# Routed attention and expert kernel: weight scaling and row turning moved between slots, expert steps written out with transposing loads

## The chip, the cores and the metric

The kernel runs on one core of one Trainium2 chip. The metric is the time of one execution on the device, in microseconds (us), less is better.

## What is computed

```python
h = tok(x)                 # 32 batches of 125 tokens x 192; the 88 with the best score are kept
h = h + attn(layernorm(h)) # 12 heads of 16, values rounded to whole steps, integer softmax
h = h + ffn(layernorm(h))

def ffn(x):                # 16 experts, each 192 -> 2 x 192 -> 192, 4 of them for each of 2816 tokens
    t = rmsnorm(x) * scale
    vals, idx = top_k(t @ gate_w.T + gate_b, 4)
    full_w = scatter(softmax(vals) / 4, idx)
    h = swiglu(einsum('th,ehf->tef', t, w1) + b1)
    y = einsum('tei,eih->teh', h, w2) + b2
    return x + einsum('teh,te->th', y, full_w) * 4
```

## The kernel before, in words

All is written out by hand: each engine has one list of instructions and semaphores, and each executes its own list in order. There are three stages.

**Start.** x is loaded, scored and the kept tokens are gathered (to about 95 us).

**Attention slots.** The tokens are NT = 24 tiles of 128 rows, three tiles to a quad of four batches (NQ = 8). `tile_slots` calls `slot(st, ...)` for st = 0 to 29 on every engine. A slot takes one tile's scores through the integer softmax: VectorE makes S_w (L1227), ScalarE S_g (L827), VectorE S_rho and S_pow (L1264, L1267), ScalarE a Square (L851), VectorE S_e and its sum (L1302, L1306), ScalarE Ln and Exp (L876, L881), VectorE S_ratio, S_rb and S_p (L1244 to L1253, in the next slot), TensorE transposes of S_p (L1593, L1598), ScalarE copies to pTs (L858, L861), TensorE pO (L1631), ScalarE o8 (L837), POOL a cast to oq (L651), TensorE the projection (L1618), VectorE the residual (L1277). Other work is laid into the slots by i = st % 3:
- q, k and v of the next quad. `project_qk` (L1486) fills bank pX, `quant_qk` (L771) on ScalarE empties it, and POOL casts it (L610). Six of these (qk 0 to 5) lie at i = 0 and 1, the v parts at i = 2.
- Expert weights in pairs: SP loads a pair into stage0 or stage1 (L442), `scale_pair` on ScalarE scales them (L720 to L726, at i = 1), `high_bias` and `high_w1` (L733 to L744) make the float16 high parts, POOL the low parts (`low_pair`, L537, at i = 0).
- Routing of a finished quad: `norm_rows` (L1128), `high_rows` (L784), low halves on POOL (L313, L314), then at st = 7 + 3q (i = 1) `turn_rows` (L1530) transposes the rows into pX in two parts, which VectorE copies (`evac_rT`, L1142); `last_rows` (L791) on ScalarE; the gate's product `gate_rows` (L1545) and `top_experts` (L1151 to L1163); and at i = 2 the ranks (L1555) and `find_slots`. POOL sends the rows to their places in `region` in HBM (L622), 12 DMAs to a quad.

All who use bank pX take it in the order of `fill_order`: each filler waits until the one before was emptied (`xr_drained`). How many sends POOL makes in a slot is given by `room`:

```python
room = 5 if st == NT else len(queue) if st > NT else (1, 6, 5)[st % 3]
```

**Expert stage.** `region` holds the rows by expert in blocks of STEP = 256. NS = 59 steps each take one block: SP loads it (`load_step`, L477 to L481, four buffers xb), TensorE transposes it into tp_ps (L1690), ScalarE copies that to xTb and its tail to tEb (L929, L930), TensorE makes the hidden layer, three windows of five products (L1681), ScalarE applies the gate function (L920, L923), VectorE clamps the other half (L1379, L1382) and multiplies (L1410), ScalarE and VectorE split the result into high and low parts (L914, L915, L1389, L1390), TensorE makes ten products (L1705), ScalarE copies them out (L908), POOL sends the result rows with two indirect DMAs (L686) to `expert_rows`. VectorE works out their addresses from 16 words behind each row (L1398, L1414). `step_slots` writes the first 16 steps and the last ones out and runs the 40 between as a loop of UNROLL = 8; TensorE reads the experts' numbers at the start of every eight (`load_experts`).

At the end the result rows are loaded again and summed on VectorE (L1428).

## Time and profile before

| | |
|---|---|
| runs | 790.51 us median of 3 (790.07 to 792.04) |
| profiled execution | 788.26 us, its span 786.5 us |
| busy, share of the span | PE 52%, PE weight loads 36%, DVE 79%, ACT 70%, POOL 56% |
| attention slots | about 98 to 499 us |
| sends of rows, tables | to 540 us |
| expert stage | 545 to 745 us |
| result rows summed | 751 to 783 us |

PE is TensorE's matmul, PEld its weight load, DVE is VectorE, ACT ScalarE, POOL GpSimd, SP SyncE; SPq is SP's DMA queue. A row of a timeline gives the start, the duration and the instruction (line, output <- inputs, shape), and in brackets how long the engine stood idle before it and for whom. "arena" is one large buffer in which many tiles lie.

### The profile page before, as it was taken

How to read it: one execution, taken by the hardware profiler on the slowest of the kernel's cores; microseconds unless marked ns; L12 is line 12 of the kernel's file. 1: busy time of each engine (PE TensorE's matmuls, PEld its weight loads, DVE VectorE, ACT ScalarE, POOL GpSimd, SP SyncE). 2: the span in 40 equal slices, each digit the busy share in tenths (PEclk: the TensorE clock that was granted, in tenths of full speed). 3: DMA queues.
4: the chain of work that ended last, by engine and by line, in shares of the span. 5: the costliest groups of instructions: out<-in, count | busy, mean ns of one | idle time of the engine just before them, and what ended most of it. 6: DMA issues, size and time to landing. Idle time of an engine off the chain costs nothing. (4 is left out here: it accounts for less than half of the span.)

```text
span 786.5 us, 16017 instructions
## 1 busy us (share of the span) xinstructions
PE 408.7 (52%) x4141; PEld 279.9 (36%) x4142; DVE 624.7 (79%) x1844; ACT 546.8 (70%) x914; POOL 437.5 (56%) x542
## 2 busy tenths in 40 slices
PE   0377545553434444544534332322999999999400
PEld 0123213232222232322312222211777777878300
DVE  3686478989599598796995988775998888888378
ACT  0235289998878788778788876426998899889300
POOL 9543263735417558378287386774366566666600
PEclk9999655555555555555555555555999999999655
DMA  8479999688201102002000001123344443333095
GB/s 185 52 166 321 319 318 296 200 264 258 60 1 39 58 24 72 25 24 85 11 24 30 29 5 49 64 79 90 94 126 122 118 121 111 108 114 98 3 380 209
DMA packets 102400, 93.47 MB, mean 119 GB/s; under 512 B 14822, under 2 KB 96493, under 8 KB 102338
## 3 DMA queue, kind: packets, MB, share of 16 engines
q1 hardware_dynamic: 88938, 72.87, 33.5%
q0 software_dynamic: 10272, 17.70, 6.5%
q10 hardware_dynamic: 3128, 2.16, 0.9%
q8 instruction: 28, 0.46, 0.2%
q14 instruction: 34, 0.28, 0.1%
...
## 5 line engine op out<-in xcount | busy, mean ns | idle before, releaser
L686 POOL DMA_INDIRECT expert_rows<-stage,dest x118 | 116.3, 985 | 85.8 <-DVE dest L1414 64.8
L622 POOL DMA_INDIRECT region<-rows,slots x60 | 65.4, 1090 | 17.8 <-issue 14.0
L1486 PE MATMUL pX<-arena,WA 128*128 128x384 f16 x86 | 35.3, 514 | 66.2 <-ACT arena L771 63.5
L537 POOL TENSOR_TENSOR w1s<-stage,w1s 128x384 f16<-128x384 f32 (+8 forms) x72 | 56.4, 784 | 9.6 <-ACT w1s L744 4.6
L1593 PE MATMUL pP<-idb,S_p 128*88 128x128 bf16 x192 | 25.8, 315 | 65.5 <-DVE S_p L1253 65.5
L1705 PE MATMUL pX<-w2s,stage 128*128 x472 | 56.8, 251 | 4.3 <-ACT stage L908 2.6
L651 POOL CAST oq<-o 128x384 bf16<-128x384 int8 x24 | 19.3, 804 | 68.7 <-ACT o L837 68.5
L1593 PEld LDWEIGHTS pP<-idb,S_p 128*88 128x88 bf16 x192 | 21.9, 191 | 70.8 <-DVE S_p L1253 68.8
L610 POOL CAST arena<-arena 128x384 bf16<-128x384 int8 x42 | 25.5, 614 | 38.1 <-ACT arena L771 37.8
L914 ACT ACTIVATE stage<-arena 128x512 f16<-128x512 f32 x59 | 37.2, 630 | 13.4 <-DVE arena L1410 12.2
L827 ACT ACTIVATE S_g<-S_w,kf 128x1056 int16<-128x1056 uint16 x24 | 30.3, 1264 | 21.6 <-DVE S_w L1227 21.6
L1410 DVE SCALAR_TENSOR_TENSOR arena<-arena 128x256 f32<-128x256 f32 x118 | 44.2, 416 | 0.0
L622 POOL DMA_INDIRECT region<-arena,slots x36 | 37.9, 1052 | 10.6 <-issue 8.7
L1705 PEld LDWEIGHTS pX<-w2s,stage 128*128 128x128 f16 x472 | 39.3, 98 | 10.6 <-issue 8.2
L1379 DVE TENSOR_SCALAR arena<-pP 64x256 f32<-64x256 f32 x59 | 25.1, 426 | 20.9 <-PE pP L1681 19.4
L1690 PE MATMUL pO<-idh,arena 128*128 128x128 f16 x354 | 30.0, 222 | 20.8 <-DMA arena<-region 19.4
L537 POOL TENSOR_TENSOR w2s<-stage,w2s 128x384 f16<-128x384 f32 (+2 forms) x24 | 37.9, 1579 | 1.9
L1302 DVE SCALAR_TENSOR_TENSOR S_e<-S_sq,kf,S_pow 128x1056 f32<-128x1056 f32 x24 | 33.7, 1405 | 5.3 <-ACT S_sq L851 5.3
L1264 DVE SCALAR_TENSOR_TENSOR S_rho<-S_g,kf,S_w 128x1056 int16<-128x1056 int16 x24 | 36.8, 1533 | 0.0
L1142 DVE COPY early<-pX 128x768 f16<-128x768 f16 (+1 forms) x16 | 7.3, 457 | 37.0 <-PE pX L1530 37.0
L1244 DVE TENSOR_TENSOR S_ratio<-S_sq,esum 128x1056 uint16<-128x1056 f32 x24 | 33.0, 1375 | 3.9 <-ACT S_sq L881 3.9
L1508 PE MATMUL pS<-arena 32*96 32x88 bf16 (+1 forms) x576 | 32.5, 274 | 4.4 <-ACT S_u L777 2.7
...
## 6 DMA issues: line engine op xcount, KB each, us to landing
...
expert_rows<-stage,dest POOLq DMA_INDIRECT x118
```

The source lines that it names most:

```text
L537: pool.tensor_tensor(ws[rows, min(kind + 1, 3), two, to:to + width], st[rows, :, at:at + width], ws[rows, kind, two, to:to + width], ALU.s ...
L622: pool.indirect_dma_start(region_rows, bass.IndirectOffsetOnAxis(ap=slots[q % 3][:, i, m:m + 1], axis=0), rows[q % 3][:, i, :].bitcast(I16 ...
L686: pool.indirect_dma_start(y_dram, bass.IndirectOffsetOnAxis(ap=dest[(st - 7) % 8][:, j:j + 1], axis=0), ysb[b][:, j, :], None, bounds_chec ...
L914: act.activation(av[b][:, 0:3:2, :], act_f[b], ACT.Copy).then_inc(s["hi_ready"], 1)
L1244: dve.tensor_tensor(S_ratio[:, :, :], S_sq[:, :, :], esum1[:, :].unsqueeze(2).broadcast_to([128, H, KEEP]), ALU.mult).then_inc(s["ratio_re ...
L1264: dve.scalar_tensor_tensor(S_rho[:, :, :], S_g[:, :, :], k(K_X), S_w[:, :, :], ALU.mult, ALU.subtract).then_inc(s["rho_ready"], 1)
L1302: dve.scalar_tensor_tensor(S_e[:, :, :], S_sq[:, :, :], k(K_KK), S_pow[:, :, :].bitcast(BF16), ALU.add, ALU.mult).then_inc(s["e_ready"], 1)
L1410: dve.scalar_tensor_tensor(act_f[f][part, m, :], gsig[r][part, m, :], G7, lin[r][part, m, :], ALU.min, ALU.mult).then_inc(s["a_ready"], 1)
L1486: ins = pe.matmul(bank[:, 0:384], W[:, 128 * c:128 * c + 128], xT[:, kind, :], start=kind == 0, stop=kind == 2)
L1508: ins = pe.matmul(pS[rows, j, KEEP * c:KEEP * c + KEEP], qT[r][blk, c, at:at + m], kT[r][blk, c, MAIN * b:MAIN * b + KEEP], start=True, st ...
L1593: ins = pe.transpose(pP[0:KEEP, 0, 128 * h:128 * h + 128], S_p[:, h, :].bitcast(BF16), idb[:, :])
L1705: ins = pe.matmul(y_ps[:, j, :], lhs, w2s[:, kind, bass.ds(k_, 1), :].rearrange("p o f -> p (o f)"), start=n == 0, stop=n == 4)
```

## The change

In the attention: `scale_pair` is split into `scale_bias`, now at i = 0, and `scale_w1`, now at i = 2; qk 3 is emptied right behind qk 2; the routed rows take bank pX before qk 4 and the gate before qk 5; VectorE's bn_stats stands between its two copies of the turned rows; POOL sends 1, 4 and 7 rows instead of 1, 6 and 5. In the expert stage: the loop is gone, all steps are written out, and the experts' numbers are read into eight registers once; the tile is loaded by a transposing DMA straight into xTb, which has eight buffers (four in the tiles of the softmax, four in the arena), and the 16 words behind each row by a second DMA, two rows to a partition; TensorE's transposes, their bank and ScalarE's large copy are gone, the tail is copied from xTb; VectorE's two clamps become one operation, and so do its two products; the two small sums with an accumulator become one operation, and a reduce takes the place of the cast. Since a partition now has two neighbouring rows' addresses, the high and low parts are written with even rows first.

```diff
-xb = [carve([2, ROW], I16, 2) for _ in range(4)]
+meta = [carve([2, 16], I16, 2) for _ in range(UNROLL)]
+xTa = [carve([3 * STEP], I16, 2) for _ in range(4)]
...
-xTb = [buf[:, :, :].rearrange("p a b -> p (a b)").bitcast(F16)[:, 0:3 * STEP].rearrange("p (k n) -> p k n", k=3)
-       for buf in (S_g, S_rho, S_pow, S_ratio)]
+xTb = [buf[:, :, :].rearrange("p a b -> p (a b)").bitcast(I16)[:, 0:3 * STEP].rearrange("p (k n) -> p k n", k=3)
+       for buf in (S_g, S_rho, S_pow, S_ratio)] + [buf.rearrange("p (k n) -> p k n", k=3) for buf in xTa]
...
-tp_ps = pO[:, 0:3 * STEP // 2].bitcast(F16).rearrange("p (k n) -> p k n", k=3)
...
         order += [(st, "qk", 2), (st, "qk", 3)] if i == 1 else []
-    if nxt:
-        order += [(st, "x", 2)] if i == 0 else [(st, "qk", 4)] if i == 1 else [(st, "v", 1)]
+    if nxt and i != 1:
+        order += [(st, "x", 2)] if i == 0 else [(st, "v", 1)]
     if quad_at(st, RANK) is not None:
...
         order += [("rows", quad_at(st, TURN), m) for m in range(2)]
+    if nxt and i == 1:
+        order += [(st, "qk", 4)]
+    if quad_at(st, GATE) is not None:
+        order += [("gate", quad_at(st, GATE))]
     if nxt and i < 2:
         order += [(st, "qk", 5 * i)]
-    if quad_at(st, GATE) is not None:
-        order += [("gate", quad_at(st, GATE))]
 return {name: 11 + n for n, name in enumerate(order)}
...
-room = 5 if st == NT else len(queue) if st > NT else (1, 6, 5)[st % 3]
+room = 5 if st == NT else len(queue) if st > NT else (1, 4, 7)[st % 3]
...
 COLUMNS = ((0, FF, 0), (FF + CA, 2 * FF, FF), (FF, FF + CA, 2 * CA))
-def step_slots(eng, begin, slot):
-    last = NS // UNROLL
-    for st in range(2 * UNROLL):
-        if st % UNROLL == 0:
-            begin(st // UNROLL)
+def step_slots(eng, slot):
+    for st in range(NS + 7):
         slot(st, st, st // UNROLL)
-    with eng.Fori(2, last) as it:
-        begin(it)
-        for u in range(UNROLL):
-            slot(2 * UNROLL + u, it * UNROLL + u, it)
-    for st in range(UNROLL * last, NS + 7):
-        if st % UNROLL == 0:
-            begin(st // UNROLL)
-        slot(st, st, st // UNROLL)
 ROUTE_CONSTS = 38
+def by_half(full):
+    return full.rearrange("p k (n j) -> p k j n", j=2)
 def active(st, lag):
...
 def load_step(st, p, it):
-    b = st % 4
+    b = st % UNROLL
     if st >= NS:
         return
-    k = sp.value_load(tabi[0:1, 1, bass.ds(p + 8, 1)], min_val=0, max_val=NBLK)
-    if st >= 4:
-        sp.wait_ge(s["tp_filled"], p - 3)
-        sp.wait_ge(s["dest_ready"], p - 3)
-    sp.dma_start(xb[b], region[bass.ds(k, 1)].rearrange("o (j p) c -> p (o j) c", p=128)).then_inc(step_loaded[b], 16)
+    _, (k,) = nc.values_load_multi_w_load_instructions(
+        tabi[0:1, 1, st + 8:st + 9], [mybir.EngineType.SP], min_val=0, max_val=NBLK,
...
+    if st >= UNROLL:
+        sp.wait_ge(s["hl_ready"], p - (UNROLL - 1))
+        sp.wait_ge(s["te_copied"], p - (UNROLL - 1))
+        sp.wait_ge(s["dest_ready"], p - (UNROLL - 1))
+    sp.dma_start(xTb[b], region[bass.ds(k, 1), :, 0:2 * C].rearrange("o n c -> (o n) c"),
+                 transpose=True).then_inc(step_loaded[b], 16)
+    sp.dma_start(meta[b], region[bass.ds(k, 1), :, 2 * C:ROW].rearrange("o (p j) c -> p (o j) c", j=2),
+                 allow_slow_non_contiguous=True).then_inc(meta_loaded[b], 16)
 for b in range(4):
...
+def scale_w1(r):
+    st = stage_in[r]
...
         quant_qk(q + 1, 2, fill(st, "qk", 2))
-    if i == 1 and st <= 19:
-        scale_pair(q * 80 + 80 * (3 - (st // 3 + 1) % 2), (st // 3 + 1) % 2)
+    if nxt and i == 1:
+        quant_qk(q + 1, 3, fill(st, "qk", 3))
     if i == 2 and st <= 20:
+        scale_w1((st // 3 + 1) % 2)
         high_bias(q + 1, q * 2 + 2, (st // 3 + 1) % 2)
...
         high_w1(q * 2, st // 3 % 2)
+    if i == 0 and st <= 18:
+        scale_bias(q * 80 + 80 * (3 - (st // 3 + 1) % 2), (st // 3 + 1) % 2)
     if st < NT:
...
         act.activation(S_sq[:, :, :], S_rho[:, :, :], ACT.Square, bias=k(K_NB2)).then_inc(s["sq_ready"], 1)
-    if nxt and i == 1:
-        quant_qk(q + 1, 3, fill(st, "qk", 3))
     if 1 <= st <= NT:
...
                        ACT.Copy).then_inc(s["pTs_ready"], 1)
-    if nxt and i == 1:
-        quant_qk(q + 1, 4, fill(st, "qk", 4))
     if i == 2 and st // 3 + 2 < NQ:
...
         last_rows(quad_at(st, TURN))
+    if nxt and i == 1:
+        quant_qk(q + 1, 4, fill(st, "qk", 4))
     if quad_at(st, COEFFS) is not None:
...
     if active(st, 3):
-        act.wait_ge(s["a_ready"], p * 2 - 4)
+        act.wait_ge(s["a_ready"], p - 2)
         if st >= 7:
             act.wait_ge(s["mm2_done"], p - 6)
-        act.activation(av[b][:, 0:3:2, :], act_f[b], ACT.Copy).then_inc(s["hi_ready"], 1)
-        act.activation(avE[b][0:CB, :], act_f[b][0:CB, 1, :], ACT.Copy).then_inc(s["ave_ready"], 1)
+        act.activation(av[b][:, 0:3:2, :].rearrange("p k (j n) -> p k j n", j=2), by_half(act_f[b]),
+                       ACT.Copy).then_inc(s["hi_ready"], 1)
+        act.activation(avE[b][0:CB, :].rearrange("p (j n) -> p j n", j=2), by_half(act_f[b])[64:128, 1],
+                       ACT.Copy).then_inc(s["ave_ready"], 1)
     if active(st, 2):
-        act.wait_ge(s["h_ready"], p * 3 - 5)
+        act.wait_ge(s["h_ready"], p * 2 - 3)
         if st >= 4:
         act.activation(gsig[r][:, 0, :], hidG[r], ACT.Gelu_apprx_sigmoid,
                        scale=1.0 / (XS * WS)).then_inc(s["gs_ready"], 1)
-        act.activation(gsig[r][0:CB, 1, :], hidC[r][0:CB, :], ACT.Gelu_apprx_sigmoid,
+        act.wait_ge(s["h_ready"], p * 2 - 2)
+        act.activation(gsig[r][64:128, 1, :], hidC[r][0:CB, :], ACT.Gelu_apprx_sigmoid,
                        scale=1.0 / (XS * WS)).then_inc(s["gs_ready"], 1)
     if active(st, 0):
-        act.wait_ge(s["tp_filled"], p + 1)
+        act.wait_ge(step_loaded[u], it * 16 + 16)
         if st >= 4:
-        act.activation(xTb[st % 4], tp_ps, ACT.Copy).then_inc(s["tp_drained"], 1)
-        act.activation(tEb[st % 4][0:CB, :], tp_ps[0:CB, 2, :], ACT.Copy).then_inc(s["te_copied"], 1)
+            act.wait_ge(s["hl_ready"], p - 3)
+        act.activation(tEb[st % 4][0:CB, :], xTb[u][0:CB, 1, :].bitcast(F16), ACT.Copy).then_inc(s["te_copied"], 1)
 for q in range(NQ):
...
         norm_x(q + 2)
-    if quad_at(st, TURN) is not None:
-        evac_rT(quad_at(st, TURN), 1)
     if 3 <= st < NT + 3:
...
         dve.bn_stats(stb[:, m, :], xsel[:, m, :]).then_inc(s["stats2"], 1)
+    if quad_at(st, TURN) is not None:
+        evac_rT(quad_at(st, TURN), 1)
     if quad_at(st, COEFFS) is not None:
...
 def expert_values(st, p, it):
...
-        dve.wait_ge(s["h_ready"], p * 3 - 4)
+        dve.wait_ge(s["hl_ready"], p - 1)
+        dve.wait_ge(s["gs_ready"], p * 2 - 2)
...
-            dve.wait_ge(s["a_ready"], p * 2 - 6)
-        dve.tensor_scalar(lin[r][0:CB, 1, :], hidC[r][64:128, :], -6.0 * XS * WS, 8.0 * XS * WS, ALU.max,
-                          ALU.min).then_inc(s["l_done"], 1)
-        dve.wait_ge(s["h_ready"], p * 3 - 3)
-        dve.tensor_scalar(lin[r][:, 0, :], hidL[r], -6.0 * XS * WS, 8.0 * XS * WS, ALU.max,
+            dve.wait_ge(s["a_ready"], p - 3)
+        dve.tensor_scalar(lin[r], hidLC[r], -6.0 * XS * WS, 8.0 * XS * WS, ALU.max,
...
-        dve.tensor_tensor(av[g][:, 1, :], act_f[g][:, 0, :], av[g][:, 0, :], ALU.subtract).then_inc(s["lo_ready"], 1)
-        dve.tensor_tensor(av[g][64:128, 2, :], act_f[g][0:CB, 1, :], av[g][0:CB, 2, :],
+        parts, halves = av[g].rearrange("p k (j n) -> p k j n", j=2), by_half(act_f[g])
+        dve.tensor_tensor(parts[:, 1], halves[:, 0], parts[:, 0], ALU.subtract).then_inc(s["lo_ready"], 1)
+        dve.tensor_tensor(parts[0:CB, 2], halves[64:128, 1], parts[64:128, 2],
...
-        dve.wait_ge(step_loaded[b], it * 32 + 16 * ((u - 1) // 4) + 16)
+        dve.wait_ge(meta_loaded[m], it * 16 + 16 * ((u - 1) // UNROLL) + 16)
...
-        for j in range(2):
-            ins = dve.scalar_tensor_tensor(rkj[o][:, j, :], meta[:, j, 0:TOPK], own[:, bass.ds(p - 1, 1), j],
-                                           meta[:, j, TOPK:2 * TOPK], ALU.is_gt, ALU.add,
-                                           accum_out=rk[o][:, j:j + 1])
-        ins.then_inc(s["rk_done"], 1)
+        dve.scalar_tensor_tensor(rkj[o][:, :, 0:TOPK], tags[:, :, 0:TOPK], own[:, st - 1:st],
+                                 tags[:, :, TOPK:2 * TOPK], ALU.is_gt, ALU.add).then_inc(s["rk_done"], 1)
...
-        for m, part in enumerate((slice(0, 128), slice(0, CB))):
-            dve.wait_ge(s["gs_ready"], p * 2 + (m - 3))
-            dve.wait_ge(s["l_done"], p * 2 - 2)
-            dve.scalar_tensor_tensor(act_f[f][part, m, :], gsig[r][part, m, :], G7, lin[r][part, m, :], ALU.min,
-                                     ALU.mult).then_inc(s["a_ready"], 1)
+        dve.wait_ge(s["l_done"], p - 1)
+        dve.scalar_tensor_tensor(act_f[f], gsig[r], G7, lin[r], ALU.min, ALU.mult).then_inc(s["a_ready"], 1)
...
-        dve.tensor_copy(dest[(st - 1) % 8][:, :], rk[o][:, :]).then_inc(s["dest_ready"], 1)
...
+        with nc.allow_low_precision(reason="sums of whole numbers below two to the power of 24"):
+            dve.tensor_reduce(dest[(st - 1) % 8][:, :], rkj[o][:, :, :], AX, ALU.add).then_inc(s["dest_ready"], 1)
...
-    if nxt and i == 1:
-        project_qk(q + 1, 4, fill(st, "qk", 4))
...
+    if nxt and i == 1:
+        project_qk(q + 1, 4, fill(st, "qk", 4))
...
+    if quad_at(st, GATE) is not None:
+        gate_rows(quad_at(st, GATE))
...
-    if quad_at(st, GATE) is not None:
-        gate_rows(quad_at(st, GATE))
...
-        pe.wait_ge(s["tp_drained"], p - 1)
+        b = (st - 2) % UNROLL
+        pe.wait_ge(step_loaded[b], it * 16 + 16 * ((u - 2) // UNROLL) + 16)
...
-            for n, (kind, rhs) in enumerate(((0, x3[:, 0, :]), (0, x3[:, 1, :]), (1, x3[:, 0, :]),
-                                             (2, x3[:, 2, :]), (3, tail[:, :]))):
+            for n, (kind, rhs) in enumerate(((0, x3[:, 0, :]), (0, x3[:, 2, :]), (1, x3[:, 0, :]),
+                                             (2, x3[:, 1, :]), (3, tail[:, :]))):
...
-            ins.then_inc(s["h_ready"], 1)
-    if active(st, 0):
-        pe.wait_ge(step_loaded[b], it * 32 + 16 * (u // 4) + 16)
-        if st >= 1:
-            pe.wait_ge(s["te_copied"], p)
-        for j in range(2):
-            for kind, lo in enumerate((0, 2 * CA, CA)):
-                ins = pe.transpose(tp_ps[:, kind, 128 * j:128 * j + 128], xb[b][:, j, lo:lo + 128].bitcast(F16), idh[:, :])
-        ins.then_inc(s["tp_filled"], 1)
+            ins.then_inc(s["hl_ready" if dst is hidL[r] else "h_ready"], 1)
```

What moves, first on ScalarE in a slot with i = 1 (slot 10): behind o8 come before

```order
L837 ACTIVATE o8<-pO,kf 128x384
L771 ACTIVATE arena<-pX,qkB,qkA 128x384
L720 ACTIVATE stage1<-stage1 64x2x192
L721 ACTIVATE stage1<-stage1 64x2x192
L722 ACTIVATE stage1<-stage1,one_ws 64x2x192
L724 ACTIVATE stage1<-stage1 128x2x384
L726 ACTIVATE stage1<-stage1,fs 128x2x384 x2
L851 ACTIVATE S_sq<-S_rho,kf 128x1056
L771 ACTIVATE arena<-pX,qkB,qkA 128x384
L858 ACTIVATE pTs<-pP 88x1024
L861 ACTIVATE pTs<-pP 88x512
L771 ACTIVATE arena<-pX,qkB,qkA 128x384
```

and of the change

```order
L847 ACTIVATE o8<-pO,kf 128x384
L781 ACTIVATE arena<-pX,qkB,qkA 128x384 x2
L864 ACTIVATE S_sq<-S_rho,kf 128x1056
L869 ACTIVATE pTs<-pP 88x1024
L872 ACTIVATE pTs<-pP 88x512
L801 ACTIVATE tEr<-early 64x384
L781 ACTIVATE arena<-pX,qkB,qkA 128x384
L887 ACT_TABLE_LOAD
```

The arena rows from pX are qk 2, 3 and 4: the six scalings are gone from between the first two, and qk 4 now comes behind the copy to tEr.

On TensorE in the same slot (qk 3, S_p, qk 4, rows, projection) before

```order
L1486 MATMUL pX<-arena,WD 128x384
L1593 MATMUL pP<-idb,S_p 88x128 x8
L1598 MATMUL pP<-idb,S_p 88x128 x4
L1486 MATMUL pX<-arena,WA 128x384 x2
L1486 MATMUL pX<-arena,WD 128x384
L1530 MATMUL pX<-idh,rows0 128x128 x9
L1618 MATMUL pP<-WpT,oq 128x192 x3
```

and of the change

```order
L1492 MATMUL pX<-arena,WD 128x384
L1599 MATMUL pP<-idb,S_p 88x128 x8
L1604 MATMUL pP<-idb,S_p 88x128 x4
L1536 MATMUL pX<-idh,rows0 128x128 x9
L1492 MATMUL pX<-arena,WA 128x384 x2
L1492 MATMUL pX<-arena,WD 128x384
L1624 MATMUL pP<-WpT,oq 128x192 x3
```

The transposes of the routed rows (rows0) have moved ahead of qk 4.

## Rows read from the trace of the kernel before

**Rows 1.** Busy time by stretches: stretch, busy time of each engine (xinstructions), PEclk, DMA share, GB/s.
```profile
600.00:650.00 50.00, 46.99 (x484) 38.57 (x484) 42.42 (x173) 44.37 (x109) 30.25 (x32) 1.00 0.41 118
```

**Rows 2.** Chain of waits of the expert stage, shares by line.
```profile
by line: PE pS L1681 30.4%; PE pX L1705 20.6%; PE pP L1681 14.0%; PE pO L1690 8.1%; issue 6.3%; DVE xsel L1428 3.9%; DMA w1s<-expert_rows 2.0%; DVE arena L1410 1.2%; ACT avE L915 1.1%; DMA arena<-region 1.1%; DMA region<-rows,slots 1.1%; AC
```

**Rows 3.** Timeline of ScalarE, slots 10 to 12: start us, us, instruction [idle before].
```profile
251.14 1.27 ACT L827 ACTIVATE S_g<-S_w,kf 128x1056 int16<-128x1056 uint16 x1 [0.17 <-DVE S_w L1227]
...
255.06 0.52 ACT L720 ACTIVATE stage<-stage 64x384 f32<-64x384 f32 x1
...
259.98 0.65 ACT L771 ACTIVATE arena<-pX,qkB,qkA 128x384 int8<-128x384 f32 x1
...
273.77 1.27 ACT L827 ACTIVATE S_g<-S_w,kf 128x1056 int16<-128x1056 uint16 x1 [2.58 <-DVE S_w L1227]
...
281.93 0.68 ACT L765 ACTIVATE arena<-arena 128x576 f16<-128x576 f32 x1 [0.62 <-DVE arena L1072]
...
285.46 1.17 ACT L876 ACTIVATE S_sq<-S_e,kf 128x1056 f32<-128x1056 f32 x1 [1.33 <-DVE S_e L1302]
...
289.48 1.27 ACT L827 ACTIVATE S_g<-S_w,kf 128x1056 int16<-128x1056 uint16 x1 [0.35 <-DVE S_w L1227]
...
294.41 1.18 ACT L851 ACTIVATE S_sq<-S_rho,kf 128x1056 f32<-128x1056 int16 x1 [0.62 <-DVE S_rho L1264]
...
298.85 0.69 ACT L784 ACTIVATE rows<-tn 128x576 f16<-128x576 f32 x1 [1.87 <-DVE tn L1128]
```

**Rows 4.** Timeline of VectorE, slot 10.
```profile
263.56 0.56 DVE L1142 COPY early<-pX 128x768 f16<-128x768 f16 x1 [6.13 <-PE pX L1530]
...
264.77 0.36 DVE L1142 COPY early<-pX 128x384 f16<-128x384 f16 x1 [0.66 <-PE pX L1530]
...
269.52 0.21 DVE L1151 COPY arena<-pX 128x48 f32<-128x48 f32 x1 [1.16 <-PE pX L1545]
```

**Rows 5.** Timeline of TensorE, slot 10.
```profile
260.69 0.82 PE L1486 MATMUL pX<-arena,WA 128*128 128x384 f16 x2 [3.18 <-ACT arena L771]
```

**Rows 6.** Timeline of POOL, slot 10: the rows' low halves.
```profile
254.64 1.92 POOL L314 TENSOR_TENSOR rows<-tn,rows 128x384 f16<-128x384 f32 x1
```

**Rows 7.** Timeline of VectorE, slot 1.
```profile
117.91 1.32 DVE L1302 SCALAR_TENSOR_TENSOR S_e<-S_sq,kf,S_pow 128x1056 f32<-128x1056 f32 x1 [3.77 <-ACT S_sq L851]
```

**Rows 8.** Timeline of SP: loads of expert pair 2.
```profile
114.28 5.96 SPq L442 DMA_DIRECT2D stage<-in_L_ffn_w_dram  x6
```

**Rows 9.** Timeline of POOL: last sends of routed rows.
```profile
536.67 0.97 POOL L622 DMA_INDIRECT region<-rows,slots  x1 [0.30 <-issue]
...
539.25 0.97 POOL L622 DMA_INDIRECT region<-rows,slots  x1 [0.30 <-issue]
```

**Rows 10.** Timeline of TensorE, expert stage: transposes of a step, and what follows.
```profile
553.06 0.50 PE L1690 MATMUL pO<-idh,arena 128*128 128x128 f16 x6
553.39 0.60 PE L1681 MATMUL pS<-S_pow,w1s 128*128 128x256 f16 x4
...
584.82 0.50 PE L1690 MATMUL pO<-idh,arena 128*128 128x128 f16 x6
...
587.72 0.50 PE L1690 MATMUL pO<-idh,arena 128*128 128x128 f16 x6
...
591.77 0.49 PE L1690 MATMUL pO<-idh,arena 128*128 128x128 f16 x6
...
725.22 0.50 PE L1690 MATMUL pO<-idh,arena 128*128 128x128 f16 x6
```

**Rows 11.** Timelines of ScalarE and VectorE, expert stage.
```profile
656.93 0.79 ACT L929 ACTIVATE S_g<-pO 128x768 f16<-128x768 f16 x1
...
657.65 0.75 DVE L1410 SCALAR_TENSOR_TENSOR arena<-arena 128x256 f32<-128x256 f32 x2
```

**Rows 12.** DMA queues (packets, MB, share of 16 engines), and the first tile load.
```profile
q1 hardware_dynamic: 88938, 72.87, 33.5%
...
q10 hardware_dynamic: 3128, 2.16, 0.9%
...
542.67 2.49 DMA arena<-region
```

More of the change, by code:

```diff
@@ L298, in audio_tower @@
         row_sent = [sem(f"row_sent{i}") for i in range(3)]
-        step_loaded = [sem(f"step_loaded{i}") for i in range(4)]
+        meta_loaded = [sem(f"meta_loaded{i}") for i in range(UNROLL)]
+        step_loaded = [sem(f"step_loaded{i}") for i in range(UNROLL)]
         y_sent = [sem(f"y_sent{i}") for i in range(4)]
@@ L1649, in _ @@
             pe.matmul(tab_ps, ones_h[:, :], tdiag[:, :, :], start=True, stop=True).then_inc(s["tabs_spread"], 1)
-            pe.wait_ge(s["own_ready"], 2)
+            pe.wait_ge(s["own_ready"], 1)
             pe.wait_ge(s["tabs_ready"], 2)
             pe.wait_ge(s["stage_low"], 12 * E // 2)
-            words = [None, None]
-            def load_experts(it):
-                _, values = nc.values_load_multi_w_load_instructions(
-                    packw[0:1, bass.ds(it, 2)], [mybir.EngineType.PE],
-                    skip_runtime_bounds_check_because="each of the eight fields of four bits is cut out before it is used")
-                words[:] = values
@@ L1663, in expert @@
-            def expert(u, lag):
-                word, field = (words[1], u - lag) if u >= lag else (words[0], u - lag + UNROLL)
-                return (word >> (4 * field)) & (E - 1)
+            _, words = nc.values_load_multi_w_load_instructions(
+                packw[0:1, 1:9], [mybir.EngineType.PE],
+                skip_runtime_bounds_check_because="each of the eight fields of four bits is cut out before it is used")
+            def expert(n):
+                return (words[n // 8] >> (4 * (n % 8))) & (E - 1)
```

67 lines of the change are left out of this document (35 added, 32 removed).

## The prediction

> **What bounds the kernel now.** I read the busy time by stretches first, then the chain of waits of the expert stage, then the timelines of one slot of the attention and one expert step. In the expert stage TensorE is busy 46.99 of 50 us at a granted clock of 1.00, the upper of its two levels [rows 1]. So the expert stage is set by TensorE's work, and its chain says so: TensorE's lines hold 73% of it [rows 2]. In the attention no engine is full all the time; there ScalarE and VectorE hand the score tile to each other, and I look for idle VectorE.
>
> That idle time is in one slot of three. The start of S_g marks a slot. In [rows 3] slot 10 lasts 251.14 to 273.77 = 22.63 us, slot 11 lasts to 289.48, 15.7. Slot 10 is one in which routed rows are turned (7, 10, 13, 16, 19 are the five that also project the next quad). VectorE stands 6.13 us before it can copy the turned rows, 0.66 between the two copies, and 1.16 for the gate's logits, 7.95 in all [rows 4]. Why are the rows late? They share bank pX with the projections qk 3 and qk 4 and come behind both. ScalarE, which must empty qk 3, first does the six scaling operations that start at 255.06 and a Square and reaches qk 3 at 259.98 [rows 3]; TensorE has waited 3.18 us for it when it starts qk 4 at 260.69 [rows 5], and the transposes of the rows come only behind that.
>
> **The attention after.** ScalarE empties qk 3 right after qk 2; of the scalings, whose 4.2 us stand between 255.06 and the Square, the bias and w2 part (2.45) goes to the slot before, the w1 part (1.7) to the slot after; TensorE turns the rows before qk 4, and the gate comes before qk 5. I walk slot 10 with the durations of [rows 3 to 5]:
> - ScalarE: qk 3 from about 256.2 (TensorE fills it 1.1 us after qk 2 is emptied) to 256.9, then Square to 258.0, the two pTs copies to 259.5.
> - TensorE: transposes of S_p from 256.2 to 257.7 (they now wait behind qk 3, as before). POOL must have made the rows' low halves by then: it ended at 256.56 [rows 6], and will end 1.1 us later (see below), at 257.7. First turn 257.8 to 258.6.
> - VectorE: idle from 257.4 to 258.7, first copy, then bn_stats (moved between the copies, so 0.36 of the 0.66 is used), second copy ends 260.2, S_e 260.3 to 261.6, esum to 263.1. Gate's logits are ready by then; its small operations end at 265.1, then the maximum and S_w end at 267.7.
> - ScalarE: the tEr copy ends 260.9, qk 4 is emptied by 262.0, table load, Ln 263.4 to 264.5, qk 5, table load, Exp ends 267.6.
> So S_g of slot 11 starts at 267.8 instead of 273.77: the slot is 16.7 long, **5.9 us less, five times: 29.5 us**. Bounds: if only TensorE's wait of 3.18 us for qk 3 went [rows 5], 16 in all; if all 7.95 us of idle time went, 40. I take 5.9, from the walk. What is late next: ScalarE and VectorE end together, and no queue is behind them by more than 0.1.
>
> The moved scalings: in slot 12 ScalarE is idle 0.62 + 1.87 us at places behind the new four; in slot 11 0.62 + 1.33 behind the new ones of w1 [rows 3]. These cover 2.45 and 1.7 us to within 0.1. They cover nothing in slots 1 to 5, where ScalarE is full: slots 1 and 4 lose 4.2 us of scaling (VectorE waited 3.77 there for the Square [rows 7]), slots 0, 2, 3 and 5 get 0.7 + 1.7 + 2.45 + 1.0. Net **-2.4** (bounds -5 and +3). The staged weights are now wanted one slot earlier: the tightest is pair 2, whose loads were issued from 114.28 on [rows 8] and are wanted at about 142, so nobody waits.
>
> POOL: the sends of a triple of slots go 1, 4, 7 instead of 1, 6, 5. Two sends (2.58 from 536.67 to 539.25 [rows 9]) move to the third slot, and push the low weights and then the low rows of the next triple by about 1.1 us; that is in the walk above. In slot 22, whose rows come from POOL in the same way, it costs 0.7; two sends moved past slot 22's idle POOL start the final run of sends about 1 us later; 0.1 in each of eight other slots. **+2.5** in all (bounds +1 and +5). POOL sends back to back up to 540.2 [rows 9], so the expert stage starts when the attention lets it end: all of this shifts it one for one.
>
> **The expert stage.** Before, TensorE issues 15 + 10 products and 6 transposes in a step. In the middle of a block of eight steps start 2.90 apart (584.82 to 587.72); where a block begins, with its register loads and branch, it is 4.05 (to 591.77). From the third step to the last, 553.06 to 725.22, 56 steps take 172.2: **3.07 a step** [rows 10]. The change takes the transposes away (553.06 to 553.39: 0.33), the loop, and ScalarE's evacuation of the turned tile (0.79). What is left:
> - TensorE 2.90 - 0.33 = 2.57.
> - POOL, two sends: 2.58 [rows 9]; its work does not change.
> - VectorE: of its six groups of operations a step, the two clamps become one of 512 columns, the two products (0.75 together [rows 11]) become one, and the two small sums with an accumulator become one and a reduce. It kept up with 2.90 before, so less than that is left; I take 2.4 (bounds 2.1 and 2.8).
> - ScalarE: it too kept up with 2.90, and loses 0.79 [rows 11]: 2.1; the copy of the tail stays.
> - SP: one more DMA a step, 32-byte pieces, 256 of them, next to the tile's load, which took 2.49 from issue to landing when nothing else was under way [rows 12]. Eight loads may be under way instead of four, so this latency is hidden as long as the loads keep pace.
> TensorE and POOL, both near 2.58, wait for each other a little: I take **2.65**. 56 x (3.07 - 2.65) = **-23.5**. Bounds: 2.56 gives -28.5 (less than POOL's row, if some pairs of sends go faster); on the other side see the rivals. The stage starts without six transposes and the 0.79 copy, but with a turning load whose latency no row shows: between 2.49 and twice that. **-1** (bounds -2.1 and +1). The combination of rows afterwards does not change.
>
> The turning load is the one price that the trace does not have. Lower bound: the plain load's. By packets: 88938 packets took 33.5% of 16 engines over 786.5 us, 47 ns each [rows 12]; if a load is cut into 768 pieces, one per row and per third of xTb, instead of 256 rows, that is 48 per engine, 2.3 us, still under 2.65. Upper bound: if the writing side cuts the 196 KB into pieces of 32 bytes, like those of the second DMA, each at the price of the small packets of queue q10 (3128 in 0.9%, 36 ns), 384 per engine are 13.9 us a step. I take the lower end: it is the nearest row, of the same bytes between the same two places, and everything up to 2.65 is hidden. A rule of the Trainium skill speaks for this end: "Advanced Engine Details and Errata", X-Bar Transpose (TRN2), says that transposing DMAs are as fast as regular ones on this chip. By that rule the sum stands as above, and by the rule under A it would be some 1030; no row here shows either.
>
> **Sum.** -29.5 - 2.4 + 2.5 - 23.5 - 1 = -53.9 against the profiled execution's 788.3 (span 786.5 and 1.8 around it), 734.4; the median of the runs is 2.2 higher, so **737 us**. A measurement of this kernel tells some 0.3% (2.4 us) from no change.
>
> **Rivals.**
> - A, the turning load becomes the bound, slower. With eight buffers the loads' own rate, not their latency, sets the step. The gain of the attention, 30 us, is used up at a step of 3.07 + 30/56 = 3.6 us. If reading and turning do not overlap, a load is worth twice the 2.49 us row, 5.0 a step: 56 x 1.93 = +108, with the attention's -30 gives 868 us. For it: the nearest price by packets has an upper end of 13.9. Against it: only 0.41 of the DMA engines are busy in this stage [rows 1]. The Trainium skill has a rule for this side too: "VectorE: DVE Perf Modes", The three transpose paths, gives 1309 ns for a 128 x 128 tile by DMA against 390 on TensorE. Six tiles one after the other would be an estimated 7.9 us a step and some 1030 us; I read the figure as the latency of one tile, since TensorE's six transposes of a step take 0.33 us here, far under that page's 390 ns each. Chance 0.17.
> - B, loads or SP's issue in between, 3.4 us a step: 56 x 0.33 = +18, 779 us. SP would then be the queue with two issues and a table load per step. Chance 0.10, most of it faster.
> - C, the attention gives half: the rows still come late since POOL's low rows end near 257.7 in any case and every later slip of POOL goes into VectorE's wait. Five slots of 3 us instead of 5.9: 752 us. For it: POOL is the queue with the least room. Chance 0.15.
> - D, the expert stage gains but the change does nothing in the attention, as ScalarE is only given its work elsewhere: against it stand the idle times of [rows 3]. It is in C's lower tail.
>
> **Chances.** Forecast 0.58, A 0.17, B 0.10, C 0.15. The forecast's own range is 724 (attention -36, step 2.56) to 750. To leave out no more than 2 in 10 the range must hold C and part of B, not A: 724 to 775. Faster: 0.58 + 0.15 + 0.08 = 0.81; slower 0.17; same 0.02.
>
> **What would show it.** In the profile after: slots 7, 10, 13, 16 and 19 near 16.7 us from S_g to S_g and VectorE's idle time before its copy of the turned rows near 1 instead of 6 us; the slots between within 0.3 of what they were; the last send of rows near 511; expert steps 2.6 to 2.7 apart without the long one at every eighth; TensorE and POOL both above 90% busy. It is wrong if TensorE's products wait for the DMA of the tiles, if the granted clock falls under 1.00 in that stage because of such waits, or if slots 11 and 12 grow by what slot 10 loses.

## The result, and the profile after

The changed kernel takes **822.54 us** (median of 4 runs, 820.95 to 823.11), the one before 790.77 in the same comparison: ratio 1.0397, interval [1.0377, 1.0416]. The forecast was 737, faster; it was slower by 32 us. The profiled execution's span is 820.7 us against 786.5.

Where did 34.2 us of span come from? I cut both traces at the same four events: the last send of rows, ScalarE's first and last copy of a tile's tail (the instruction that ends a step on its queue), and the last send of results.

| | before | after | |
|---|---|---|---|
| last send of rows starts | 539.25 | 507.55 | **-31.7** |
| from it to the first tail copy | 7.58 | 6.32 | -1.3 |
| first to last tail copy, 58 steps | 179.92 (3.10 each) | 240.88 (4.15) | **+61.0** |
| last tail copy to last send of results | 17.06 | 21.86 | +4.8 |
| from there to the end | 42.7 | 44.1 | +1.4 |

So the attention gave what was forecast, and the expert stage, forecast at 2.65 us a step, went to 4.25 (the 4.15 of the table is the mean with the shorter first steps). The timeline of POOL in the changed kernel, against [rows 9]:

```profile
507.55 0.97 POOL L624 DMA_INDIRECT region<-rows,slots  x1 [0.30 <-issue]
```

**The attention.** ScalarE's timeline at S_g, slots 10, 11, 13 and 14, against [rows 3], then VectorE's at its copies of the turned rows in slots 10 and 13, against [rows 4]:

```profile
244.38 1.27 ACT L837 ACTIVATE S_g<-S_w,kf 128x1056 int16<-128x1056 uint16 x1 [0.17 <-DVE S_w L1238]
...
260.65 1.25 ACT L837 ACTIVATE S_g<-S_w,kf 128x1056 int16<-128x1056 uint16 x1
...
290.45 1.25 ACT L837 ACTIVATE S_g<-S_w,kf 128x1056 int16<-128x1056 uint16 x1
...
308.57 1.25 ACT L837 ACTIVATE S_g<-S_w,kf 128x1056 int16<-128x1056 uint16 x1
```

```profile
251.43 0.56 DVE L1153 COPY early<-pX 128x768 f16<-128x768 f16 x1 [0.76 <-PE pX L1536]
...
252.65 0.36 DVE L1153 COPY early<-pX 128x384 f16<-128x384 f16 x1 [0.40 <-PE pX L1536]
...
299.55 0.56 DVE L1153 COPY early<-pX 128x768 f16<-128x768 f16 x1 [2.61 <-PE pX L1536]
```

Slot 10 is 16.27 long instead of 22.63. Slots 13, 16 and 19 are 18.1: there VectorE still waits 2.6 us for the rows. POOL's timeline before slot 13's copy shows the low halves ending at 298.6, with a send ahead of them:

```profile
295.96 1.20 POOL L624 DMA_INDIRECT region<-rows,slots  x1 [0.80 <-POOL w2s L539]
297.23 0.54 POOL L314 TENSOR_TENSOR rows<-tn,rows 128x192 f16<-128x192 f32 x1
297.73 0.90 POOL L315 TENSOR_TENSOR rows<-tn,rows 128x384 f16<-128x384 f32 x1
```

**The expert stage.** The busy time by stretches, the same stretch as [rows 1]:

```profile
600.00:650.00 50.00, 32.25 (x292) 24.00 (x290) 27.51 (x69) 29.96 (x72) 22.43 (x23) 1.00 0.48 92
```

No engine is busy for more than two thirds of the time, the DMA engines for half, and TensorE's clock is still granted in full. Nothing is the bottleneck as an engine; something waits in a circle. The costliest groups of the page name it (busy us, mean ns, then idle time ahead and its releaser):

```profile
L691 POOL DMA_INDIRECT expert_rows<-stage,dest x118 | 115.7, 981 | 151.2 <-ACT stage L919 127.7
L1391 DVE TENSOR_SCALAR arena<-pS 128x512 f32<-128x512 f32 x59 | 40.8, 691 | 110.1 <-issue 103.1
L1698 PE MATMUL pX<-w2s,stage 128*128 x472 | 59.3, 254 | 89.1 <-DVE stage L1399 82.4
...
L925 ACT ACTIVATE stage<-arena 128x512 f16<-128x512 f32 x59 | 39.2, 664 | 96.5 <-DVE arena L1416 96.5
```

POOL waits for ScalarE, TensorE for VectorE, ScalarE for VectorE's product (L1416), and VectorE stands 1.87 us before each clamp (L1391). Waits for loads are few: those of ScalarE's tail copies add up to 8.2 us and fall on the stage's first loads. The timelines of one step, VectorE's and then ScalarE's, close the circle:

```profile
640.01 0.69 DVE L1391 TENSOR_SCALAR arena<-pS 128x512 f32<-128x512 f32 x1 [1.83 <-issue]
640.62 0.41 DVE L1399 TENSOR_TENSOR stage<-arena,stage 128x256 f16<-128x256 f32 x1
641.06 0.42 DVE L1400 TENSOR_TENSOR stage<-arena,stage 64x256 f16<-64x256 f32 x1
641.52 0.23 DVE L1408 SCALAR_TENSOR_TENSOR rkj<-arena,own 128x8 f32<-128x8 f32 x1
641.66 0.68 DVE L1416 SCALAR_TENSOR_TENSOR arena<-arena 128x512 f32<-128x512 f32 x1
642.26 0.15 DVE L1420 TENSOR_REDUCE dest<-rkj 128x2 int32<-128x10 f32 x1
644.25 0.69 DVE L1391 TENSOR_SCALAR arena<-pS 128x512 f32<-128x512 f32 x1 [1.84 <-issue]
```

```profile
642.38 0.66 ACT L925 ACTIVATE stage<-arena 128x512 f16<-128x512 f32 x1 [1.65 <-DVE arena L1416]
643.06 0.43 ACT L927 ACTIVATE avE<-arena 64x256 f16<-64x256 f32 x1
643.40 0.36 ACT L933 ACTIVATE arena<-pP 128x256 f32<-128x256 f32 x1
643.79 0.38 ACT L936 ACTIVATE arena<-pS 64x256 f32<-64x256 f32 x1
```

VectorE's product ends at 642.34, ScalarE's two copies of its high part begin at 642.38, behind them on ScalarE's queue come the two gelus of the next step, which end at 644.17, and VectorE's clamp of that step begins at 644.25. 2.33 + 0.04 + 1.79 + 0.08 = 4.24 us, the step. The page calls VectorE's wait "issue", not ScalarE, so the releaser had to be found in the code:

```diff
-dve.wait_ge(s["h_ready"], p * 3 - 4)
+dve.wait_ge(s["hl_ready"], p - 1)
+dve.wait_ge(s["gs_ready"], p * 2 - 2)
 ...
-dve.tensor_scalar(lin[r][0:CB, 1, :], hidC[r][64:128, :], ...)
+dve.tensor_scalar(lin[r], hidLC[r], ...)
```

`gs_ready` counts ScalarE's gelus. Before, VectorE waited for it only ahead of its products, the last large operations of its step. Why does the wait stand before the clamp now? The clamp uses nothing that the gelus make. But the joined clamp reads all 128 partitions of the bank hidC, of which ScalarE's second gelu reads partitions 0 to 63; before, each engine read its own half. The Trainium skill, "PSUM — Partial Sum Buffer", PSUM bank collisions raise a hardware error, says that two engines must not be in one bank and one group of 32 partitions at the same time, not even to read. That the wait is there for this rule is my reading of the code. No run here shows such a collision; what the traces show is the price of the wait.

### The profile page after: what moved, and what is told of

Same layout as the page of the kernel before. It is cut to its first block and busy times, and to the rows that moved or that the text cites. A ratio compares the mean times of both kernels' runs of the same rounds, so it can differ in the third digit from the quotient of the medians.

```text
span 820.7 us, 14116 instructions
## 1 busy us (share of the span) xinstructions
PE 393.9 (48%) x3787; PEld 257.0 (31%) x3787; DVE 596.3 (73%) x1547; ACT 526.4 (64%) x855; POOL 430.4 (52%) x544
## 5 line engine op out<-in xcount | busy, mean ns | idle before, releaser
L1391 DVE TENSOR_SCALAR arena<-pS 128x512 f32<-128x512 f32 x59 | 40.8, 691 | 110.1 <-issue 103.1
L1698 PE MATMUL pX<-w2s,stage 128*128 x472 | 59.3, 254 | 89.1 <-DVE stage L1399 82.4
L925 ACT ACTIVATE stage<-arena 128x512 f16<-128x512 f32 x59 | 39.2, 664 | 96.5 <-DVE arena L1416 96.5
L624 POOL DMA_INDIRECT region<-rows,slots x60 | 62.6, 1044 | 17.8 <-issue 14.2
L539 POOL TENSOR_TENSOR w1s<-stage,w1s 128x384 f16<-128x384 f32 (+8 forms) x72 | 61.6, 855 | 6.0 <-ACT w1s L753 0.8
L1624 PE MATMUL pP<-WpT,oq 128*128 128x192 bf16 x72 | 15.6, 354 | 57.8 <-ACT pTs L872 57.8
L781 ACT ACTIVATE arena<-pX,qkB,qkA 128x384 int8<-128x384 f32 x43 | 28.5, 664 | 18.6 <-PE pX L1492 18.3
L1416 DVE SCALAR_TENSOR_TENSOR arena<-arena 128x512 f32<-128x512 f32 x59 | 40.3, 684 | 0.0
L1434 DVE SCALAR_TENSOR_TENSOR xsel<-w1s,W,xsel 128x192 f32<-128x192 f32 x64 | 21.4, 413 | 18.5 <-DMA w1s<-expert_rows 18.5
```

The lines of the kernel that those rows point to most:

```text
L539: pool.tensor_tensor(ws[rows, min(kind + 1, 3), two, to:to + width], st[rows, :, at:at + width], ws[rows, kind, two, to:to + width], ALU.s ...
L624: pool.indirect_dma_start(region_rows, bass.IndirectOffsetOnAxis(ap=slots[q % 3][:, i, m:m + 1], axis=0), rows[q % 3][:, i, :].bitcast(I16 ...
L925: act.activation(av[b][:, 0:3:2, :].rearrange("p k (j n) -> p k j n", j=2), by_half(act_f[b]), ACT.Copy).then_inc(s["hi_ready"], 1)
L1391: dve.tensor_scalar(lin[r], hidLC[r], -6.0 * XS * WS, 8.0 * XS * WS, ALU.max, ALU.min).then_inc(s["l_done"], 1)
L1416: dve.scalar_tensor_tensor(act_f[f], gsig[r], G7, lin[r], ALU.min, ALU.mult).then_inc(s["a_ready"], 1)
L1434: dve.scalar_tensor_tensor(xsel[:, n, :], ybuf[n][:, C * m:C * m + C], W4[:, n, m:m + 1], xsel[:, n, :], ALU.mult, ALU.add).then_inc(s["co ...
```

## The experiments

My theory after reading: this ring alone makes the step 4.25 us, and everything else of the change is worth what was forecast. The rival: the turning load or SP's issue of it.

**gelus_first.** ScalarE's gelus ahead of its copies, in each step:

```diff
 def gate_values(st, p, it):
 ...
+    if active(st, 2):  # the two gelus, L933 and L936
+        ...
     if active(st, 3):  # the two copies, L925 and L927
         ...
-    if active(st, 2):
-        ...
```

> The changed kernel; ScalarE's two gelus of a step are placed ahead of its two copies of the high parts of the step before. Nothing is left out. Theory 1 (the ring: VectorE's merged clamp waits for both gelus, the gelus stand behind the high copies, those wait for VectorE's product of the step before, 2.4 + 1.8 us = the 4.25 us step): the ring is cut, since a gelu no longer stands behind a product of the step before; the step falls to what engines or the next loop set, 2.6 to 3.0 us, and the time from 822.5 by 56 x 1.25 to 1.6 to 732 to 752. Theory 2 (the turning load or SP's two issues set the 4.25 us): nothing there changes, 822 +- 3. Theory 3 (the whole ring of buffers, copies and sends is too tight): 3.4 to 4.0 us a step, 775 to 808.

Measured: **735.33 us**, ratio to the kernel before 0.9286 [0.9271, 0.9302]. The wait before the clamp is still there, but a gelu no longer stands behind a product. The same stretch as above:

```profile
600.00:650.00 50.00, 49.86 (x461) 37.64 (x459) 42.91 (x110) 46.49 (x111) 37.87 (x37) 1.00 0.71 140
```

TensorE is full, and a step takes 2.74 us on average (VectorE's clamps at 599.66, 602.46 and 605.10; the 59 of them from 517.25 to 676.34). Theory 1 holds: two blocks of code exchanged, 87 us.

**clamp_split.** The other way to cut the ring: the clamp in two, as before the change.

```diff
+dve.wait_ge(s["h_ready"], p * 2 - 2)
-dve.wait_ge(s["hl_ready"], p - 1)
-dve.wait_ge(s["gs_ready"], p * 2 - 2)
-dve.tensor_scalar(lin[r], hidLC[r], ...)
+dve.tensor_scalar(lin[r][64:128, 1, :], hidC[r][64:128, :], ...)
+dve.wait_ge(s["hl_ready"], p - 1)
+dve.tensor_scalar(lin[r][:, 0, :], hidL[r], ...)
 ...
+dve.wait_ge(s["gs_ready"], p * 2 - 2)
 dve.scalar_tensor_tensor(act_f[f], gsig[r], G7, lin[r], ALU.min, ALU.mult)
```

> The changed kernel, but the clamp is two operations again, each waiting only for its own window, and the wait for the gelus stands before the product, as before the change; unused halves of the clamped tile are zeroed once. Nothing is left out. Theory 1 (the ring through the clamp's wait for the gelus): VectorE does clamps, subtractions and sums while ScalarE does the gelus; what is left of the ring is product, two copies, two gelus, some 2.6 to 2.9 us; VectorE has one operation more (0.35 us). Step 2.7 to 3.1, 738 to 760. Theory 2 (load or SP's issue): 822 +- 3. Theory 3: 775 to 808.

Measured: 737.08 us, 0.9302 [0.9286, 0.9317]. The same within 2 us, and a step takes 2.75 to 2.76 us, since VectorE now works without a pause. This kernel keeps the old order on ScalarE, so it differs from gelus_first in two things; that joining the clamps is worth next to nothing is likely, but no run changes it alone.

**before_with_wait.** The suspected wait put into the kernel before, and nothing else:

```diff
 dve.wait_ge(s["h_ready"], p * 3 - 4)
+dve.wait_ge(s["gs_ready"], p * 2 - 2)
```

> The kernel before with one wait more: VectorE's first clamp of a step also waits for both gelus of that step. Nothing is left out. Theory 1 (that wait alone makes the ring): the step goes from 3.07 to about 4.4 us (two clamps, two subtractions, two sums, two products, some 2.6 us on VectorE, and 1.8 on ScalarE), 790.8 + 56 x 1.3 = 864, at least 845. Theory 2 (load): the wait costs little, under 800. Theory 3 (it needs the merged operations too): 800 to 845.

Measured: 866.69 us (2 runs, 863.57 and 869.80), 1.0939 [1.0891, 1.0987]. Most of its steps are 4.36 long, and here the trace names the releaser, the second gelu:

```profile
625.44 0.42 DVE L1380 TENSOR_SCALAR arena<-pP 64x256 f32<-64x256 f32 x1 [1.55 <-ACT arena L923]
...
627.43 0.75 DVE L1411 SCALAR_TENSOR_TENSOR arena<-arena 128x256 f32<-128x256 f32 x2
...
629.80 0.43 DVE L1380 TENSOR_SCALAR arena<-pP 64x256 f32<-64x256 f32 x1 [1.55 <-ACT arena L923]
```

One line makes the ring without any turning load, joined operation or written-out step. This settles the cause.

**attention_alone.** The attention's hunks of the change on the kernel before.

> The kernel before with the attention's part of the change alone (scalings split and moved, qk 3 emptied sooner, rows ahead of qk 4, the gate ahead of qk 5, bn_stats between the copies, 1, 4, 7 sends); its expert stage is the one before the change. Theory: the two parts add up. The last send of rows came 31.7 us sooner in the changed kernel, so 790.8 - 31.7 = 759, expert step 3.07 as before. Rival (the expert stage's start hides part of it, or the attention gained only together with the freed queue work): 765 or more.

Measured: 760.0 us, 0.958 [0.9561, 0.9599]. The parts add up: -32 for the attention, and with the ring cut another -25 for the expert stage (760.0 to 735.3).

**loop_written_out.** attention_alone with its looped steps written out:

```diff
-for st in range(2 * UNROLL): ...
-with eng.Fori(2, last) as it: ...
-for st in range(UNROLL * last, NS + 7):
+for st in range(NS + 7):
```

> The kernel of attention_alone (expert stage as before the change, with TensorE's transposes) with its 40 looped steps written out; the experts' numbers are still read at every eighth step. Nothing is left out. In attention_alone eight steps take 25.6 us (588.15 to 613.75 on TensorE), 3.2 each, with 4.3 and 3.4 where a block begins and 2.9 in its middle. Theory 1 (the loop's boundary costs what the long steps show; transposes cost 0.3 of the 2.9): eight steps of 2.95, 40 x 0.25 = 10 us less, 760 - 10 = 750, range 746 to 753; the turning loads and the joined operations are then worth the other 15 us to 735.3. Theory 2 (the boundary is the register loads, which stay): 757 to 760.

Measured: 816.08 us, beside 844.66 for the kernel before, where that one took 790.1 to 793.8 in all the other comparisons. It was another chip. In this run's trace VectorE's and ScalarE's operations of the expert stage have their usual durations, but its steps vary from 2.84 to 6.74 us past the first few, 3.86 on average. The cause of the longer waits I did not find. The ratio, 0.9664, cannot be set beside the others, so it was run again:

> The kernel of loop_written_out once more, since on the chip of that call the kernel before took 844.7 us instead of 792 and every expert step had stalls that its own trace does not explain. As before: theory 1 (the loop's boundary costs what the long steps show) 746 to 753; theory 2 (it is the register loads, which stay) 757 to 760, both where the kernel before takes about 792.

Measured: 751.6 us, 0.9493 [0.9476, 0.9511], the kernel before at 791.7; a step takes 3.00 on average. The loop's boundary is worth 8 us. The other 16 of the expert stage's 25 are a difference, not a run: they hold the turning loads, the joined operations, the order of the gelus and the experts' numbers read once.

**plain_loads.** gelus_first with a load that does not turn; what it leaves out is the turning, so its experts compute on rows that are not transposed:

```diff
-sp.dma_start(xTb[b], region[bass.ds(k, 1), :, 0:2 * C].rearrange("o n c -> (o n) c"), transpose=True)
+sp.dma_start(xTb[b].rearrange("p k n -> p (k n)").rearrange("p (j c) -> p j c", j=2),
+             region[bass.ds(k, 1), :, 0:2 * C].rearrange("o (j p) c -> p (o j) c", p=128))
```

> The kernel of gelus_first with a plain load of the same 196 KB in the place of the turning load (what it leaves out: the turning, so the experts work on rows that are not transposed; every instruction on the engines stays). In gelus_first TensorE is busy 49.9 of 50 us from 600 us on, and SP issues one step's loads every 2.5 us at the stage's start. Theory 1 (the turning load is hidden; TensorE sets 2.6 us): within 4 us of 735.3, 731 to 736. Theory 2 (the turning load costs in the open, in its rate or by traffic beside the sends): under 725.

Measured: 733.35 us, 0.925 [0.9227, 0.9272], against 0.9286: the turning costs the kernel 2 us or so, at the edge of what these comparisons can tell. What it costs elsewhere is in the stretch, where the DMA share is 0.53 and gelus_first has 0.71:

```profile
600.00:650.00 50.00, 49.78 (x459) 37.78 (x458) 42.90 (x111) 46.35 (x110) 38.73 (x37) 1.00 0.53 138
```

and on SP's queue, first in gelus_first:

```profile
512.53 1.23 SPq L480 DMA_TRANSPOSE S_rho<-region  x1
513.97 0.60 SPq L482 DMA_DIRECT2D arena<-region  x1
515.00 1.24 SPq L480 DMA_TRANSPOSE S_pow<-region  x1
```

and then in this run:

```profile
623.32 0.38 SPq L480 DMA_DIRECT2D arena<-region  x1
623.88 0.55 SPq L482 DMA_DIRECT2D arena<-region  x1
```

A turning load holds SP's queue for 1.23 us, a plain one for 0.38. With the second DMA and the read of the block's number from the table SP gives out one step in 2.5 us, just under the 2.74 of a step.

**turning_twice.** gelus_first with a second turning load a step, into buffers that nobody reads:

```diff
+...
+if st >= 4:
+    sp.dma_start(twice_buf[st % 4], region[bass.ds(k, 1), :, 0:2 * C].rearrange("o n c -> (o n) c"), transpose=True)
```

> The kernel of gelus_first with every turning load from the fifth on issued twice, the second into buffers that nobody reads (nothing is left out). One step's issues on SP then take 2.5 + 1.3 = 3.8 us. Theory 1 (the DMA engines have room: 0.71 busy at 2.6 us a step, SP's issue is what is scarce): step 3.8, 735.3 + 55 x 1.2 = 801, range 790 to 812. Theory 2 (the engines or the turning itself become the bound, over 2 us for one load): step over 4.2, 820 or more. Theory 3 (SP's issue runs ahead and costs nothing): under 760.

Measured: 805.6 us, 1.016 [1.0133, 1.0187]. The steps are 3.93 long on average. SP's queue holds one step for 4.0 us (606.20 to 610.22), back to back, and from 560 to 700 us SP's lines hold 73% of the chain of waits:

```profile
606.20 1.23 SPq L483 DMA_TRANSPOSE S_rho<-region  x1
607.47 1.28 SPq L490 DMA_TRANSPOSE S_sq<-region  x1
608.95 0.56 SPq L492 DMA_DIRECT2D arena<-region  x1
610.22 1.23 SPq L483 DMA_TRANSPOSE S_pow<-region  x1
```

So here the turning loads ran short of SP's queue first, and two of them went through in a step of 4.0 us: one costs at most 2.0 in rate.

**scalings_back.** gelus_first with `scale_bias` and `scale_w1` both at i = 1 again, behind qk 3.

> The kernel of gelus_first with all six scaling operations again in slots 1, 4, 7 and so on (i = 1), behind qk 3; everything else of the attention's change stays. Nothing is left out. Theory 1 (both the early qk 3 and the moved scalings matter; the six, 4.2 us, then push the Square and with it S_e, of which the rows' lateness hides some 2 us): slots 7 to 19 grow by 2 us each, slots 1 and 4 by up to 2, 735.3 + 12 = 747, range 743 to 753. Theory 2 (the order of bank pX is all of the gain): within 2.5 us of 735.3. Theory 3 (the scalings are all of it): 760 or more.

Measured: 749.24 us, 0.9458 [0.9433, 0.9482]. Slot 10 is 18.57 long (+2.3), slot 1 17.98 (+4.0, where up to 2 was expected): VectorE's S_e waits for the Square again. Slots 0, 2, 3 and 5, which no longer hold the scalings, are shorter by 0.7 to 2.3.

```profile
120.65 1.32 DVE L1313 SCALAR_TENSOR_TENSOR S_e<-S_sq,kf,S_pow 128x1056 f32<-128x1056 f32 x1 [5.67 <-ACT S_sq L864]
...
261.16 1.32 DVE L1313 SCALAR_TENSOR_TENSOR S_e<-S_sq,kf,S_pow 128x1056 f32<-128x1056 f32 x1 [2.25 <-ACT S_sq L864]
```

Of the attention's 32 us the scalings' place is worth 14. The other 18 are the difference, for the order of bank pX with what goes with it; no run has that order alone.

**sends_0_5_7 and sends_0_4_8.** gelus_first with another `room`, to take the send out from before the low rows of slots 13, 16 and 19:

```diff
-room = ... (1, 4, 7)[st % 3]
+room = ... (0, 5, 7)[st % 3]
```

> The kernel of gelus_first with POOL sending 0, 5 and 7 rows' DMAs in the three slots instead of 1, 4 and 7. In slots 13, 16 and 19 VectorE waited 2.6 us before it copied the turned rows, and POOL had made one send (with 0.8 us ahead of it) between the low weights and the low rows. Nothing is left out. Theory 1 (that send makes the rows late): three slots of about 2 us less, 735.3 - 5 = 730, range 727 to 732. Theory 2 (POOL is late either way, or the fifth send delays the casts of q and k): 734 to 738.

Measured: 737.9 us, 0.9315 [0.9293, 0.9337]. VectorE's wait for the rows fell from 12.1 to 5.7 us (from 100 to 480 us of the trace), and slot 13 by 0.9; but slot 17 grew from 14.8 to 17.3. A fifth send stands among the casts of q and k in slot 16, two of the five took 1.90 and 1.95 us instead of 0.98, and ScalarE waits for the scores:

```profile
358.89 1.14 ACT L787 ACTIVATE S_u<-pS,kf 128x1056 int8<-128x1056 f32 x1 [2.42 <-PE pS L1514]
```

With 0, 4 and 8 sends the first run fell on the chip of loop_written_out (809.97 us beside 844.66), so it too was repeated:

> The kernel of gelus_first with 0, 4 and 8 sends in the three slots. With 0, 5 and 7 the rows came sooner (VectorE waited 5.7 us for them in place of 12.1) but slots 14 and 17 grew, by 0.6 and 2.5 us. Nothing is left out. Theory 1 (the fifth send in the slot of q's and k's casts was what took it back): rows come 0.7 us sooner than with 1, 4, 7, nothing grows, 735.3 - 2 to 4 = 731 to 733.5. Theory 2 (POOL's queue is full over three slots, so what one slot gains the next gives back): 735 to 739.

> The kernel of sends_0_4_8 once more, for the same reason. Theory 1 (the fifth send beside the casts took back what 0, 5, 7 had gained): 731 to 733.5. Theory 2 (POOL's queue is full over three slots): 735 to 739. Both where the kernel before takes about 792.

Measured in the repeat: 740.31 us, 0.934 [0.9319, 0.9362], just above theory 2's range; slots 13, 16 and 19 take 18.5. Neither is faster than 1, 4, 7, as theory 2 said, and only the second is slower clear of noise. Part of both is not the sends: S_g of slot 0 begins 1.2 and 2.0 us later than in gelus_first. Theory 2's reason, a full queue, is not shown either: from 300 to 396 us POOL is busy 72.5 of 96 us in sends_0_5_7.

The fastest kernel that does the whole work is gelus_first, 735.33 us: 57 us under the kernel before in its comparison and 87 under the changed one.

## Why the prediction was wrong

**The step that failed** is the expert stage's "What is left", the terms of VectorE and ScalarE. It asked how long each engine is busy in a step and took the longest, TensorE's 2.57. For VectorE it said "it kept up with 2.90 before, so less than that is left; I take 2.4". Its busy time is indeed 2.4 (640.01 to 642.41), but the sentence counts the joined clamp as a shorter operation and never looks at what it waits for. The diff had that wait in a line of its own. What had to be asked of it: what stands behind it on VectorE's queue (everything up to the product), who waits for that (ScalarE's copies, and the gelus behind them), and does that lead back to it. It does: 2.33 + 1.79 and two handovers of 0.04 and 0.08 are 4.24 us. A ring of this size could have been estimated from the kernel before, whose trace holds the same operations of both engines. before_with_wait shows it: about 4.4 us was foretold for it and 4.36 came, though its terms were off and made up for each other: VectorE 2.74 (625.44 to 628.18) where 2.6 was taken, ScalarE 1.47 where 1.8 was the sum of its durations.

None of the rivals had it either. A was slower by the wrong mechanism (the loads), and its way of telling, TensorE's products waiting for the tiles, did not appear.

Point by point, the rest:
- **Attention**, forecast -29.4 at POOL's last send (-29.5, -2.4, +2.5): it was -31.7. The sum was right, in part by luck, since its terms were off both ways. The five slots gave 26.6 instead of 29.5, since slots 13, 16 and 19 kept a wait of 2.6 us for POOL's low halves: rival C's mechanism, at a third of its size. The eight slots between (8, 9, 11, 12, 14, 15, 17, 18), forecast unchanged, gave 5.7; slots 0 to 6 gave 0.5 instead of 2.4, since slots 1 and 4 lost 2.6 us each and not 4.2. Slots 20 to 22 gave another 0.6, the first slot began 1.2 later, and the sends behind the last S_g, forecast at most of +2.5, cost 0.5.
- **Loop, transposes, turning loads**, forecast -23.5 for the steps: with the ring cut the first and last tail copy are 158.91 us apart instead of 179.92, -21.0. A step is 2.74 on average instead of 2.65. Six of the first 20 take 3.1 to 3.4, where ScalarE's tail copy waits for a load that SP gave out late. In the middle, with TensorE busy 49.86 of 50 us, they are still 2.6 to 2.8, so TensorE's term of 2.57 was low too; why its products take longer than in the kernel before was not tested. The forecast of 737 is near what the kernel takes once the ring is cut (735.3), and the attention's 2.3 us more and the steps' 2.5 less cancel in it.
- **ScalarE**, forecast 2.1 us a step: it is 2.6 (642.38 to 644.98 in the changed kernel), and in gelus_first it is busy 46.5 of 50 us. The large copy went, but the operations that stayed follow each other more slowly than these of before_with_wait: from the first copy to the second 0.68 instead of 0.53, from gelu to gelu 0.39 instead of 0.26, though their own durations are nearly the same. Why was not tested.

```profile
623.85 0.63 ACT L914 ACTIVATE stage<-arena 128x512 f16<-128x512 f32 x1 [1.93 <-DVE arena L1411]
624.38 0.40 ACT L915 ACTIVATE avE<-arena 64x256 f16<-64x256 f32 x1
624.69 0.36 ACT L920 ACTIVATE arena<-pS 128x256 f32<-128x256 f32 x1
624.95 0.36 ACT L923 ACTIVATE arena<-pP 64x256 f32<-64x256 f32 x1
```

- **Stage start**, forecast -1: -1.3 (before: 7.58, after: 6.32 us from the last send to the first tail copy). The load's latency, bounded between 2.49 and twice that, is 3.21, where the plain load of the same bytes in plain_loads takes 2.46:

```profile
510.58 3.21 DMA S_g<-region
```

- **The turning load as a rate**, taken at its lower end: right for the time, and so was the rule of the Trainium skill, "Advanced Engine Details and Errata", X-Bar Transpose (TRN2), to within the 2 us of plain_loads. The packets went as the estimate's case of 768 pieces has it, and not the 6144 of its upper bound: q1 has 47200 more than in [rows 12], 800 for each of 59 steps, of which 768 would be these pieces. The rule under A, of the Trainium skill's "VectorE: DVE Perf Modes", The three transpose paths, 1309 ns a tile and so an estimated 7.9 us a step, does not hold as a rate: twelve such tiles a step went through in 4.0 us. As a latency of one tile it was not tested.

```profile
q1 hardware_dynamic: 136138, 72.88, 35.5%
```
